# Batched averages and stores on SyncE in a depthwise convolution followed by a rotation

## The reference

```
x = x + depthwise_conv5x5(_gn(x), kernel)       # one 5x5 kernel of 16 taps for each channel, padding 2
x = x + einsum('hvc,bchw->bvhw', R, _gn(x))     # R: a 128x128 rotation for each of the 64 rows h
```

## Time and profile before

| | |
|---|---|
| median of 3 runs | 543.72 us |
| the profiled execution's own time | 545.81 us |
| its span, first to last instruction | 544.0 us |
| PE busy | 423.9 us (78%) |
| PE weight loads | 201.9 us (37%) |
| DVE busy | 348.4 us (64%) |
| POOL busy | 334.5 us (61%) |
| ACT busy | 299.7 us (55%) |
| DMA, mean | 259 GB/s, 140.67 MB |
| granted TensorE clock, mean | 0.972 of full speed |

### The profile page before, as it was taken

One profiled execution on the slowest core, in us unless ns is written; L12 is line 12 of the kernel. 1 busy time (PEld: TensorE's weight loads), 2 busy tenths in 40 slices (PEclk: granted clock), 3 DMA queues, 4 the chain that ended last, 5 costly groups with the idle time before them and its releaser, 6 DMA issues.

```text
span 544.0 us, 8852 instructions
## 1 busy us (share of the span) xinstructions
PE 423.9 (78%) x3168; PEld 201.9 (37%) x3168; DVE 348.4 (64%) x648; ACT 299.7 (55%) x566; POOL 334.5 (61%) x416
## 2 busy tenths in 40 slices
PE   0048999989989989989989989911999867676772
PEld 0024554434444444444434444511444323233230
DVE  3226988778878878878869787740674444535353
ACT  1116666566566567566567677623677455454640
POOL 4299788878888888988889986202344323232320
PEclk9999999999999999999999999975899999999997
DMA  9998998988888988987889998958599999999998
GB/s 142 182 199 143 242 221 201 217 196 201 218 203 197 218 205 196 226 207 194 218 198 262 270 268 228 360 128 204 167 371 396 393 397 397 395 397 396 398 391 302
DMA packets 208170, 140.67 MB, mean 259 GB/s; under 512 B 140096, under 2 KB 172928, under 8 KB 208128
## 3 DMA queue, kind: packets, MB, share of 16 engines
q1 hardware_dynamic: 181200, 103.31, 68.8%
q10 hardware_dynamic: 26128, 35.28, 24.7%
q0 software_dynamic: 800, 1.54, 1.3%
HBM read 72.95 MB, written 67.13 MB: 258 GB/s over the span
## 4 chain that ended last, share of the span: by engine, by line
ACT 24%; ACTq 21%; DMA 17%; PE 13%; issue 8%; SPq 8%; DVE 5%; POOL 2%; DVEq 0%; POOLq 0%
ACT area L344 17%; DMA out_dram<-area 15%; ACTq L333 14%; PE ps L481 8%; SPq L206 7%; ACT area L360 5%; PE ps L537 4%; ACTq L327 4%; ACT std L355 2%; DVE affine L419 1%; DMA norm<-affine 1%; POOL area L268 1%; SPq L224 1%; ACTq L172 1%; DMA row_taps<-tap_rows 1%
## 5 line engine op out<-in xcount | busy, mean ns | idle before, releaser
L481 PE MATMUL ps<-area 64*64 64x512 f32 x2560 | 295.3, 601 | 13.7 <-POOL area L286 11.5
L344 ACT ACTIVATE area<-ps 64x512 f32<-64x512 f32 x256 | 150.8, 589 | 95.2 <-issue 79.5
L481 PEld LDWEIGHTS ps<-area 64*64 64x64 f32 x2560 | 138.6, 132 | 120.6 <-issue 120.6
L268 POOL TENSOR_TENSOR area<-mask,row_taps 128x325 f32<-128x325 f32 x128 | 158.0, 1267 | 23.9 <-PE ps L481 14.0
L537 PE MATMUL ps<-area 128*128 128x512 f32 x256 | 120.1, 610 | 38.9 <-DVE area L460 29.3
L460 DVE TENSOR_TENSOR area<-ps,area 128x512 f32<-128x512 f32 x128 | 81.5, 685 | 84.7 <-DMA out_dram<-area 64.9
L302 POOL TENSOR_SCALAR area<-area,norm 128x256 f32<-128x256 f32 x96 | 52.0, 555 | 130.3 <-PE ps L537 78.6
L286 POOL TENSOR_SCALAR area<-area,affine 128x256 f32<-128x256 f32 x160 | 113.0, 719 | 29.9 <-DVE affine L421 29.9
L379 ACT ACTIVATE area<-area,norm 128x256 f32<-128x256 f32 x160 | 82.0, 588 | 69.2 <-PE ps L537 47.5
L449 DVE BATCH_NORM_STATS2 stats<-area 128x6 f32<-128x512 f32 x128 | 80.6, 692 | 15.7 <-DMA area<-in_x_dram 15.7
L537 PEld LDWEIGHTS ps<-area 128*128 128x128 f32 x256 | 46.4, 193 | 101.4 <-DVE area L460 53.7
(11 more groups left out here) (23 smaller groups left out, 51.6 us busy)
## 6 DMA issues: line engine op xcount, KB each, us to landing
x_scratch<-area ACTq DMA_DIRECT2D x64, 512.0 KB, 6.5
out_dram<-area SPq DMA_DIRECT2D x32, 1024.0 KB, 11.4
area<-in_x_dram SPq DMA_DIRECT2D x244, 128.0 KB, 4.2
area<-x_scratch SPq DMA_DIRECT2D x27, 1024.0 KB, 12.6
area<-x_scratch SPq DMA_DIRECT2D x5, 896.0 KB, 11.5
area<-in_x_dram ACTq DMA_DIRECT2D x12, 128.0 KB, 7.1
row_taps<-tap_rows POOLq DMA_DIRECT2D x8, 142.2 KB, 6.5
norm<-affine ACTq DMA_DIRECT2D x64, 0.2 KB
```

The costliest lines, as they stand in the source:

```text
L268: last = nc.gpsimd.tensor_tensor(taps[k % TRING][:, c * KW:(c + 1) * KW].rearrange("p d (b r) -> p d b r", r=TAPS), bass.AP(tensor=of_rows ...
L344: last = nc.scalar.activation(y[k % YRING][rows, 2 * pair + c], ps[half, bank + n].rearrange("p (j w) -> p j w", j=J), ACT.Identity)
L481: last = nc.tensor.matmul(ps[half, bank + n], taps[k % TRING][rows, (2 * pair + c) * KW + d, 0:H], padded[k % GRING][rows, 2 * pair + c, : ...
```

## The change

- The stores of the first sum are issued by SP, in its step s after the loads of group s+5, behind a wait for `x1_ready` of group s-1.
- The scales and shifts of groups 0 to 27 go to a DRAM scratch in batches of 7 groups (two DMAs a batch, `store_norms`), issued by SP in steps 11, 18 and 25 and, the fourth, after the third of the early granule loads. One DMA then fetches all of them into `norm2`. Only groups 28 to 31 are still sent one by one by ACT. `NORM2` is 16 + 32 x 4 = 144.
- SP waits for `norm2_landed` before it loads granules 5 and 6.
- At the start POOL stores the first part of the taps and issues all 10 loads of that part; ACT stores the second part, and SP issues its 10 loads after the x loads of group 3. POOL spreads the taps of group 1 after it has normed group 0, not before.
- DVE measures x of group s+3 at the beginning of step s, not at its end, from step 4 on (`FILL`). `stats_ready` now counts the statistics of x and of the sum separately (`measured`).

```diff
--- before.py
+++ after.py
@@ -35,6 +35,9 @@
 TRING = 3
 PAIRS = 3
 ROUNDS = GROUPS + 4
+NBATCH = 7
+LAST = GROUPS - GROUPS % NBATCH
+FILL = 4
 POOL_J = 5
 
 
@@ -56,6 +59,7 @@
 def conv_rotate_kernel(nc, x, weight, rota, out):
     tap_rows = nc.dram_tensor("tap_rows", (2 * TAPS, C, KW), F32, kind="Internal").ap()
     x1_dram = nc.dram_tensor("x1_scratch", (C, H, B, W), F32, kind="Internal").ap()
+    norm2_dram = nc.dram_tensor("norm2_scratch", (C, 2, 2, J), F32, kind="Internal").ap()
     rota_src = rota.rearrange("h v c -> v h c")
 
     with ExitStack() as ctx:
@@ -121,7 +125,7 @@
         x_landed = [sem(f"x_landed{n}") for n in range(XRING)]
         near_ready = sem("near_ready")
         mask_ready = sem("mask_ready")
-        taps_landed = [sem(f"taps_landed{n}") for n in range(3)]
+        taps_landed = [sem(f"taps_landed{n}") for n in range(2)]
         taps_ready = sem("taps_ready")
         stats_ready = sem("stats_ready")
         mean_ready = sem("mean_ready")
@@ -138,6 +142,7 @@
         y_ready = sem("y_ready")
         x1_ready = sem("x1_ready")
         x1_stored = [sem(f"x1_stored{n}") for n in range(YRING)]
+        norm2_stored = sem("norm2_stored")
         norm2_landed = sem("norm2_landed")
         rot_landed = sem("rot_landed")
         in_landed = [sem(f"in_landed{n}") for n in range(IRING)]
@@ -162,16 +167,26 @@
         def granule_landings(n):
             return 16 * (n // IRING + 1) + (16 if n % IRING < EARLY else 0)
 
+        def measured(r):
+            return min(r + 1, GROUPS) + max(r - 3, 0)
+
         def is_round(r):
             return 0 <= r < ROUNDS
 
         STEPS = range(-3, GROUPS + 3)
+        NORM2 = 16 + 32 * (GROUPS - LAST)
 
         def load_half(queue, k, n):
             for c in range(GC):
                 queue.dma_start(xin[k % XRING][n * HALF:(n + 1) * HALF, :, c],
                                 x[n * J:(n + 1) * J, k * GC + c].rearrange("j h w -> h j w")
                                 ).then_inc(x_landed[k % XRING], 16)
+
+        def store_line(queue, part):
+            cs = slice(0, FIRST * GC) if part == 0 else slice(FIRST * GC, C)
+            for n in range(2):
+                queue.dma_start(tap_rows[n * TAPS:(n + 1) * TAPS, cs].rearrange("r c k -> c r k"),
+                                line[cs].rearrange("c (r k) -> c r k", r=TAPS)).then_inc(line_stored[part], 16)
 
         def load_taps(queue, part, n, landed):
             cols = slice(0, FIRST * GCK) if part == 0 else slice(FIRST * GCK, CK)
@@ -185,10 +200,29 @@
 
         @block.sync
         def _(sp):
+            def store(k):
+                for n in range(2):
+                    rows = slice(n * HALF, (n + 1) * HALF)
+                    dst = x1_dram[k * GC:(k + 1) * GC, :, n * J:(n + 1) * J, :].rearrange("c h j w -> h c (j w)")
+                    sp.dma_start(dst, y[k % YRING][rows].rearrange("p c j w -> p c (j w)")
+                                 ).then_inc(x1_stored[k % YRING], 16)
+
+            def store_norms(first):
+                groups = slice(first, first + NBATCH)
+                sp.wait_ge(affine_ready, first + NBATCH + 4)
+                for n in range(2):
+                    sp.dma_start(norm2_dram.rearrange("(g c) n k j -> c g n (k j)", c=GC)[:, groups, n],
+                                 affine[n * HALF:n * HALF + GC, first + 4:first + 4 + NBATCH, 1].rearrange(
+                                     "p g k j -> p g (k j)")).then_inc(norm2_stored, 16)
+
             for k in range(XRING - 1):
                 load_half(sp, k, 0)
                 if k >= 3:
                     load_half(sp, k, 1)
+                if k == 3:
+                    sp.wait_ge(line_stored[1], 32)
+                    load_taps(sp, 1, 0, taps_landed[1])
+                    load_taps(sp, 1, 1, taps_landed[1])
 
             for s in range(GROUPS + 3):
                 if group(s + XRING - 2) and s >= 1:
@@ -196,6 +230,11 @@
                         sp.wait_ge(x1_ready, 2 * (s - 1))
                     load_half(sp, s + XRING - 2, 0)
                     load_half(sp, s + XRING - 2, 1)
+                if group(s - 1):
+                    sp.wait_ge(x1_ready, 2 * s)
+                    store(s - 1)
+                if s > NBATCH + 3 and (s - NBATCH - 4) % NBATCH == 0 and s - NBATCH - 4 < LAST - NBATCH:
+                    store_norms(s - NBATCH - 4)
                 if s in range(ROT_STEP, ROT_STEP + ROT_LOADS):
                     n = s - ROT_STEP
                     rows = slice(n * (H // ROT_LOADS), (n + 1) * (H // ROT_LOADS))
@@ -213,6 +252,10 @@
             for n in range(EARLY):
                 sp.wait_ge(x1_ready, 2 * (XRING * ((GROUPS - 1 - EARLY_SLOTS[n]) // XRING) + EARLY_SLOTS[n] + 1))
                 load_granule(n, early).then_inc(in_landed[n], 16)
+                if n == 2:
+                    store_norms(LAST - NBATCH)
+            sp.wait_ge(norm2_stored, 32 * (LAST // NBATCH))
+            sp.dma_start(norm2[0:LAST * GC], norm2_dram[0:LAST * GC]).then_inc(norm2_landed, 16)
             for k in range(YRING):
                 sp.wait_ge(x1_stored[k], 32 * (GROUPS // YRING))
             for n in range(EARLY):
@@ -224,6 +267,7 @@
                 sp.dma_start(out[half * J:(half + 1) * J, :, u * RH:(u + 1) * RH, :].rearrange("j c h w -> c j (h w)"),
                              tout[n % ORING].rearrange("p j h w -> p j (h w)")).then_inc(out_stored[n % ORING], 16)
 
+            sp.wait_ge(norm2_landed, NORM2)
             for n in range(EARLY, IRING):
                 load_granule(n, slice(0, C)).then_inc(in_landed[n], 16)
             for n in range(GRANULES):
@@ -249,16 +293,15 @@
                 pool.wait_ge(near_ready, d + 1)
                 nc.gpsimd.affine_select(out=near[:], in_=near[:], compare_op=ALU.not_equal, fill=1.0, base=d - PAD,
                                         pattern=[[-1, HALF + BAND]], channel_multiplier=1).then_inc(near_ready, 1)
+            pool.wait_ge(line_ready, len(POS_IDX + NEG_IDX))
+            store_line(pool, 0)
             pool.wait_ge(line_stored[0], 32)
-            load_taps(pool, 0, 1, taps_landed[1])
+            load_taps(pool, 0, 0, taps_landed[0])
+            load_taps(pool, 0, 1, taps_landed[0])
             pool.wait_ge(mask_ready, 2)
 
             def spread_taps(k):
-                if k < FIRST:
-                    pool.wait_ge(taps_landed[0], 16 * TAPS)
-                    pool.wait_ge(taps_landed[1], 16 * TAPS)
-                else:
-                    pool.wait_ge(taps_landed[2], 16 * 2 * TAPS)
+                pool.wait_ge(taps_landed[0 if k < FIRST else 1], 16 * 2 * TAPS)
                 if k >= TRING:
                     pool.wait_ge(convolved, 2 * (k - TRING + 1))
                 of_rows = mask[:].rearrange("p (b r) -> p b r", r=TAPS)
@@ -275,7 +318,7 @@
                 last.then_inc(taps_ready, 1)
 
             for s in STEPS:
-                if group(s + 2):
+                if group(s + 2) and s != -1:
                     spread_taps(s + 2)
                 k = s + 1
                 if group(k):
@@ -289,11 +332,9 @@
                                                        affine[:, k, 0, 1, j:j + 1], ALU.mult, ALU.add)
                     last.then_inc(normed_pool, 1)
                 if s == -1:
-                    pool.wait_ge(line_stored[1], 32)
-                    load_taps(pool, 1, 0, taps_landed[2])
-                    load_taps(pool, 1, 1, taps_landed[2])
-
-            pool.wait_ge(norm2_landed, 32 * GROUPS)
+                    spread_taps(1)
+
+            pool.wait_ge(norm2_landed, NORM2)
             for n in range(GRANULES):
                 pool.wait_ge(in_landed[n % IRING], granule_landings(n))
                 if n >= NRING:
@@ -311,21 +352,9 @@
             nc.scalar.activation(warm[:], eps[:], ACT.Sqrt)
             load_half(act, 0, 1)
             act.wait_ge(line_ready, len(POS_IDX + NEG_IDX))
-            for part, cs in enumerate((slice(0, FIRST * GC), slice(FIRST * GC, C))):
-                for n in range(2):
-                    act.dma_start(tap_rows[n * TAPS:(n + 1) * TAPS, cs].rearrange("r c k -> c r k"),
-                                  line[cs].rearrange("c (r k) -> c r k", r=TAPS)).then_inc(line_stored[part], 16)
+            store_line(act, 1)
             load_half(act, 1, 1)
-            act.wait_ge(line_stored[0], 32)
-            load_taps(act, 0, 0, taps_landed[0])
             load_half(act, 2, 1)
-
-            def store(k):
-                for n in range(2):
-                    rows = slice(n * HALF, (n + 1) * HALF)
-                    dst = x1_dram[k * GC:(k + 1) * GC, :, n * J:(n + 1) * J, :].rearrange("c h j w -> h c (j w)")
-                    act.dma_start(dst, y[k % YRING][rows].rearrange("p c j w -> p c (j w)")
-                                 ).then_inc(x1_stored[k % YRING], 16)
 
             def send_norms(k):
                 act.wait_ge(affine_ready, k + 5)
@@ -338,7 +367,7 @@
```

(47 more changed lines are left out.)

## The result

The changed kernel takes 556.65 us (median of 4 runs, 555.54 to 557.95) against 543.86 of the kernel before in the same session. The ratio is 1.0229, 95% interval [1.019, 1.0268]. Forecast was 522.5, with 509 to 536 for the range.

A forecast was written before the change was run, and what follows sets the result against it. ACT's queue of norm DMAs and stores was taken to bound phase one's step. Step -22.4, double measurement +1.2, start -4.8, passage +4.7 gave -21.3 us: 522.5 us from a median of 543.72, range 509 to 536.

The forecast's parts named there:

- Part 4: Passage to phase two: early granule loads wait behind the last stores; +5.5, together +4.7 us (bounds +2.2 and +7.4).
- The bound before: Phase one: ACT's queue makes the step 10.16 us against PE's 8.89, 33 us in 26 steps.
- Part 1: Phase one: norm DMAs and stores leave ACT; step 9.3 us instead of 10.16, -22.4 us (bounds -33.0 and +3.7).
- (c): DMA limit per step: loads and stores in SP's one queue take 9.0 us one after the other, 8.8 overlapped.
- the sum: Whole kernel, all four parts of the change: -22.4 + 1.2 - 4.8 + 4.7 = -21.3 us.
- Part 2: DVE measures one group ahead from step 4: double measurement costs 1.2 us once (bounds 0 and 2.5), earlier x nothing.
- SP's issue becomes the bound: Rival, phase one, chance 0.09: SP's 9.0 us are real cost; step 10.3, with batches 10.5; +9.9 us, 553.6.
- My 9.1 for DVE: Phase one limit: DVE's cycle, 9.26 us measured once, 8.4 without the 0.87 beside POOL, taken as 9.1.
- Part 3: The start: group 1 ready at 42.9 us against 47.76, so -4.8 us (bounds -2.5 and -6.5).
- A: Point of reference for the passage: the last add, at 360.32 us in the kernel before.
- the dearer sum: Passage with granules at 274 GB/s: A + 5.9 + 5 x 3.35 + 2 = A + 24.6, +8.2 us.

The follow-up runs named there:

- the last experiment: The changed kernel, SP still storing, with four stores, early loads in the loop, DVE's old order and late rotations: 524.95 us, ratio 0.9616.
- the first experiment: The changed kernel with the stores of the sum issued by ACT again: 517.1 us, ratio 0.9484 to the kernel before.
- the best version: The changed kernel with the stores issued by ACT again and DVE's old order (FILL = GROUPS): 508.13 us, ratio 0.9343.

## Why the prediction was wrong

In the profiles the change was forecast at -21.3 us and came out at +12.1, 33.4 us apart. Of these, 21.7 are in the start and phase one (Parts 1 to 3), 10.7 in the passage (Part 4) and 1.0 behind it.

**The bound before: right.** ACT's norm DMAs, behind the stores in its queue, made the step 10.16 us. Taken off alone they give 512.02 us, and the step is the 8.9 of PE.

**Part 1, the step: the failed one.** I read SP's 9.0 busy us a step as 5.5 of issue and 3.5 of back-pressure that was "DMA time and already in (c)", and took 9.3 us with two stores more. SP's step measured 10.1. Where the sum had -22.4 for the 26 steps and +1.2 for Part 2, roots 3 and 29 lie 7.4 us closer than before, 255.8 us for 263.1. The 3.5 us are no slack that the engines work off in any case. Most of them are 1.3 to 1.5 us on each of two issues behind a pair of stores, and they come in whichever queue the next DMAs stand. In the timeline of the kernel before, SP's queue and then ACT's, one pair of stores at 143 us held both:

```profile
144.41 1.96 SPq L172 DMA_DIRECT2D area<-in_x_dram  x1
```
```profile
144.67 2.02 ACTq L333 DMA_DIRECT2D norm<-affine  x1
```

With the stores gone from ACT's queue, and so at other times, a norm DMA costs 0.6 as a rule. On SP the two stores' own issues come on top: 2 x 0.65 + 2.0 + 2.1 + 6 x 0.68 = 9.5, with 0.46 a step between the issues and the batches 10.1. The rival "SP's issue becomes the bound" had 10.3 and 10.5 and was the right mechanism; its 553.6 us is near the measured time partly by luck: it had phase one with the start 9.5 us too dear (the next point) and the passage 10.7 too cheap (Part 4).

**What the rival missed: a lead.** SP runs ahead by the x ring. At 10.1 against 8.9 us it is used up in some 12 steps; so the steps up to root 15 were PE's, and only then DVE waited for x (49.1 us). One more group of lead, by DVE's old order, moved that to root 22. Phase one therefore gained 5.1 us with the start, where my sum had -22.4 + 1.2 - 4.8 - 0.8 = -26.8 and the rival +4.4.

**What the sum left out: the rotation loads.** They stand in SP's queue among the last loads of x, and the sum had no term for them. The two steps after roots 28 and 29 cost 13.4 us over 8.9 each; with the rotations three steps later and SP still storing (the last experiment) no step of phase one is over 10.5.

**PE and DVE as limits.** My 9.1 for DVE was too high: with the stores on ACT and the norms in batches the step is 8.9 from root 3 to root 33. The long adds of the earlier trace rows go on, 6 of 55 with up to 2.1 us, but they don't lengthen a step; DVE's 137.4 us of 140 leave it little to spare. (c), 8.8 to 9.0 us for one step's DMAs, lengthened no step either: two queues move them in 8.9.

**Part 2: 1.2 forecast for the double measurement, 1.3 measured.** That x must be there a step earlier was put at nothing, and this was wrong: with the rotations ahead of it the x of one group comes 7.7 us late (517.1 against 508.13 us and 509.94).

**Part 3, the start: right in kind, 1.8 us too large.** Forecast -4.8, measured -3.0 at A; group 1's first convolution began at 44.91, not at 42.9. The tap stores through POOL, of which no row told, landed at 14.16, and POOL went on at 14.44 and not at 12. ACT's stores of the second part, now issued beside them, landed at 13.99; before, the first part's went ahead and had landed at 10.21. So it need not be POOL's queue that made them late. In the changed kernel's timeline:

```profile
14.44 5.78 POOL L196 DMA_DIRECT2D row_taps<-tap_rows  x10 [8.69 <-DMA tap_rows<-line]
...
26.78 4.00 POOL L311 TENSOR_TENSOR area<-mask,row_taps 128x325 f32<-128x325 f32 x4 [6.55 <-DMA row_taps<-tap_rows]
```

**Part 4, the passage: right in kind, a third of its size.** +5.5 forecast, with +8.2 (A + 24.6) as the far end, +16.2 (A + 32.6) measured. The term that was mis-sized is the transfer of the five early granules. The last store landed at 361.93, A + 6.7, where I had 5.9. The fifth granule, issued at 363.86, landed 21.5 us later:

```profile
L245 SPq DMA_DIRECT2D area<-x_scratch x2: 409/771/1133, 363.4 to 363.9; - x2
...
DMA to landing us min/median/max: 17.6/19.5/21.5
```

So the five took from 361.93 to 385.35, 23.4 us, where the dearer sum had 5 x 3.35 = 16.8 at 274 GB/s. All DMAs together went at 211 GB/s meanwhile, with a share of 103%:

```profile
DMA packets 2755, 4.94 MB, mean 211 GB/s; under 512 B 352, under 2 KB 352, under 8 KB 2755
...
q1 hardware_dynamic: 2723, 4.94, 102.8%
```

Why they ran slower than the earlier trace rows is not shown. The late part of granule 0 landed at 387.72, 2.4 us behind the fifth granule, where I had 2: its 11.1 us in the chain are nearly all time behind granules 3 and 4, and the wait for the batch ahead of it cost little. The kernel before with its stores on SP has no batch, and its passage is 33.2 us.

PE convolved until 351 us and rotated from 391 on, with some tiny matmuls between, and the granted clock was 0.50, the level of 1.2 GHz, throughout 367 to 390 us and 0.80 on average from 390 to 408. The first 8 rotation matmuls took 6.7 us where they took 5.6 before; that is about the size of the last +1.0 us.

## What to carry to other kernels

A wait in a queue that one reads as "only back-pressure" goes along when the work is moved to another queue, and lands on whatever stands behind it; before a DMA is moved, write down the target queue's own time per step, long issues included, and add to it. A ring's lead hides such a deficit for a number of steps, lead divided by deficit, so look at late steps and not at the first ones. And a store that moves into the queue of later loads brings its own wait with it: everything issued after the loop now begins after the last store. Here it was tiny DMAs behind large stores in one queue that cost ACT its time. Batching the tiny ones alone gave 512 us, with the new start 508; moving the stores instead also brought the step to 8.9 us for 20 steps, but filled SP's queue, and gave 554.

## What the hardware showed that I had not expected

- Behind two stores of 512 KB the next two DMAs take 2.0 and 2.1 us to issue, in either queue and whatever their size (a load of 128 KB, a norm DMA of 0.2 KB; of the two DMAs of a batch, 1.8 KB each, the first took 1.9 and the second 1.3 to 1.9). With stores of 256 KB it is 1.2 to 1.3 us on three. That this is the time in which a store drains fits the rate of the earlier trace rows, 0.52 MB in 2.2 us, but it isn't shown: at 335.66 us of the kernel before, with granule loads in flight, a norm DMA behind two stores took 0.65 us. What decides this stays open.
- The same loads and stores take 8.9 us a step through two queues and 10.1 through one, with the DMA engines idle for at least 13% of the time in the latter.
- A store whose outermost dimension has size 2 used 2 of 16 engines and nearly doubled the kernel's time.
- The issue of the DMA behind a rotation load took 5.26 us in the changed kernel, 5.45 in the first experiment and 10.42 in the last. In steps 24 and 25 of the best version it took 2.2 and 1.9. What decides this is open too.
